# A decoder layer with eight experts: the first expert's weights split in the attention stage, no GpSimd drain between the stages, context values by half rows

## The chip, the cores and the metric

The kernel runs on one core of a Trainium2 chip. A core has five engines, each with its own instruction stream: TensorE (PE in the profile; its weight loads are PEld), VectorE (DVE), ScalarE (ACT), GpSimd (POOL) and SyncE (SP), which here only issues DMAs. They wait for each other by semaphores. The metric is the device time of one execution in microseconds (us): 1263.66 us before, the median of 3 runs (1262.08 to 1265.37).

## The reference

The input is x, 16 sequences of 256 tokens of 256 channels, f32. Three residual parts follow one another, each after a layer norm:

1. attention within windows of 8 tokens, 16 heads of 16 channels, the sequence shifted by 4, with a relative bias;
2. cross-attention of 16 heads of 64 channels to a context of 77 rows of 192 channels per sequence;
3. a mixture of 8 experts: each token goes to the one expert with the highest router logit.

```python
qkv = xw @ w_qkv + b_qkv                      # windows of 8 tokens
attn = softmax(q @ k.T * 16**-0.5 + bias); out = (attn @ v) @ w_proj + b_proj
k = context @ Wk; v = context @ Wv            # [77,192] @ [192,1024]
attn = softmax((x @ Wq) @ k.T * 64**-0.5); out = (attn @ v) @ Wo + bo
top1 = argmax(softmax(x @ router_w + router_b))
h = x @ w1[i] + b1[i]; a, g = split(h)        # w1[i]: [256, 2048]
y = (a * sigmoid(g)) @ w2[i] + b2[i]          # w2[i]: [1024, 256]
out = out + where(top1 == i, y, 0)
```

## The kernel before

The program has two stages, each one `Block`, that is five instruction streams that start together and meet at a barrier at the end. [...]

**The first stage** (`trunk`) takes the 16 sequences in 4 groups of 4. The windows of a group lie one on each of the 128 partitions, 8 tokens a window. The scores and values of the window attention are not matmuls: for each of the 8 queries an engine multiplies q (or the probabilities) by all 8 keys (or values) into a tile of 2048 numbers per partition (`make_product`, L275), and DVE sums the tile (`sum_scores` L808, `sum_values` L837). In later groups GpSimd makes all products, in three tiles. In the opening, window group 0, DVE makes those of even queries, in `xw`, and GpSimd those of odd queries (`POOL_FIRST`), in `tmp1`: two tiles, and the semaphore `consumed` says how many have been summed.

Beside it PE, in the opening, turns the context of two sequences at a time (`turn_context` L1121), makes their keys (`keys`, L1128) and their values (`context_values`, L1139). The context has 192 channels, so a value is two matmuls over the partitions: channels 0 to 127, and channels 128 to 191 with the rest of the 128 rows zero, which GpSimd clears at L412 to L414. The results go over ACT (`pair_kept`, L638) to memory, and SP loads the keys and values of a sequence when it is due (`load_keys`, L308; `load_values`, L311). ACT rounds the keys (`round_keys`, L656) ahead of the normed tokens `xn` (L616) in its stream. PE turns the window outputs (`output_turn`, L1095) two queries at a time, as soon as these are summed, and then projects them (`project`, L1108).

Each turn of `turn` handles one sequence: scores, values, four turned outputs `o2T` (ACT, L675), output projection, router logits (`logits`), queries for the next and the maxima of their scores (`maxima`, L865). The last group has no windows to prepare. SP loads the first expert's weights into `staged` before it (L380 to L383). Each sequence ends with `store_tokens` (L495) and `scatter_ids` (L483), which scatters token numbers into the list of each expert (`ids`).

**The second stage** (`experts`) works on 23 tiles of 256 tokens; the first four take the first tile of experts 0 to 3. Weights come in three pieces of 1 MB (`w1` in two, `w2`), are staged, and are split into a high and a low part: ACT copies (`high_part`, L1706), DVE subtracts (`low_part`, L1637). SP reads the ids of a tile, GpSimd gathers its tokens (`gather`, L1536) into `xs`, which DVE clears first (L1633) because rows without a token aren't written. PE turns them (`turn_tokens`, L1779), then runs three matmuls for each product. `locate` (L1601) is a list of small DVE steps that finds which expert the tiles after the eighth belong to; SP waits for it. The tiles run in a loop (`tiles`, L1455) with the next tile's preparation inside. Scattered results are waited for by SP at L1525.

## Time and profile before

| | us |
|---|---|
| median of 3 runs | 1263.66 |
| the profiled execution | 1264.1 |
| its span, first to last instruction | 1262.3 |
| PE busy | 1150.2 (91%) |
| DVE busy | 845.1 (67%) |
| POOL busy | 656.2 (52%) |
| ACT busy | 603.3 (48%) |

The times of the stages below are microseconds from the start of the span. PE is the engine that is busy most, and its idle time lies in a few stretches: the first 41 us, some 9 us around 140, 24.6 us between the stages, 6.6 us near 865 and 12 us at the end. A busy share is an average; what a change is worth is read at the wait that ends last in its place. A row of the timeline shows in brackets how long the engine had been idle before, and what ended the wait. The profile infers the releaser, and where it names an engine that had long been done, it was another.

### The profile page before, as it was taken

To read this page: it belongs to the slowest core of one execution; us is meant where nothing else is said; L and a number is where in the kernel's file an instruction comes from. 1 tells how busy PE (TensorE), PEld (TensorE's weight loads), DVE (VectorE), ACT (ScalarE), POOL (GpSimd) and SP (SyncE) were. 2 spreads that over 40 slices of the span, in tenths; PEclk is the share of its full clock that TensorE was granted. 3 is DMA by queue.
4 is the path that set the end of the run, shared out by engine and by line. 5 is a ranking of instruction groups with operands and counts; after the bars stand their busy time and mean duration, and the time that the engine had idled before them with its cause. 6 is when DMAs were issued, how large, how long until landed. Compare 5 with 4: busy or idle time off the path is not lost. (4 is left out here: it accounts for less than half of the span.)

```text
span 1262.3 us, 22231 instructions
## 1 busy us (share of the span) xinstructions
PE 1150.2 (91%) x8064; PEld 974.3 (77%) x8064; DVE 845.1 (67%) x1501; ACT 603.3 (48%) x1003; POOL 656.2 (52%) x542
## 2 busy tenths in 40 slices
PE   4999789999998999999999999627999999999996
PEld 2666457777777777677777888527999999999995
DVE  3678356777648776577773444338788888888983
ACT  1243332445514545334455544226666676666672
POOL 6347307666538575377765221351555655555551
PEclk9999899999999999999999999858999999999998
DMA  8432301111220111201124111144666766666650
GB/s 184 133 121 105 109 20 44 46 29 46 36 61 19 36 44 25 51 13 44 29 82 115 28 34 37 33 143 144 223 236 219 242 220 231 228 209 203 219 185 1
DMA packets 95383, 133.47 MB, mean 106 GB/s; under 512 B 42394, under 2 KB 76908, under 8 KB 89411
## 3 DMA queue, kind: packets, MB, share of 16 engines
q1 hardware_dynamic: 79299, 111.30, 28.1%
q0 software_dynamic: 16000, 21.07, 6.2%
q8 instruction: 51, 0.84, 0.3%
q14 instruction: 33, 0.27, 0.1%
HBM read 113.04 MB, written 24.73 MB: 109 GB/s over the span
## 5 line engine op out<-in xcount | busy, mean ns | idle before, releaser
L1792 PE MATMUL psH<-xhigh,whigh 128*128 128x256 f32 x736 | 209.2, 284 | 8.0 <-DVE wlow L1640 6.6
L1792 PE MATMUL psH<-xlow,whigh 128*128 128x256 f32 x736 | 206.7, 281 | 0.0
L1792 PE MATMUL psH<-xhigh,wlow 128*128 128x256 f32 x736 | 206.6, 281 | 0.0
L1640 DVE TENSOR_TENSOR wlow<-staged,whigh 128x2048 fp32r<-128x2048 f32 x69 | 158.1, 2293 | 0.0
L1709 ACT ACTIVATE whigh<-staged 128x2048 fp32r<-128x2048 f32 x69 | 132.3, 1919 | 44.6 <-DMA staged<-in_L_ffn_w 27.9
L1792 PEld LDWEIGHTS psH<-xhigh,whigh 128*128 128x128 f32 x736 | 141.1, 192 | 8.9 <-issue 6.8
L1295 PEld LDWEIGHTS psD<-vo,pT 128*128 128x128 f32 x1024 | 123.9, 192 | 24.1 <-issue 20.5
L1295 PE MATMUL psD<-vo,pT 128*128 128x128 f32 x1024 | 134.0, 278 | 6.9 <-issue 5.2
L1792 PEld LDWEIGHTS psH<-xlow,whigh 128*128 128x128 f32 x736 | 140.0, 190 | 0.0
L1792 PEld LDWEIGHTS psH<-xhigh,wlow 128*128 128x128 f32 x736 | 139.7, 190 | 0.0
L1534 POOL TENSOR_TENSOR idle<-e_less 128x1 f32<-128x1 f32 x42 | 49.8, 1185 | 170.6 <-DMA ids_now<-ids 86.6
L1154 PE MATMUL psA<-xT,wq 128*128 128x256 f32 x512 | 123.1, 389 | 0.7 <-ACT xT L629 0.7
L1723 ACT ACTIVATE sig<-psH,b1s 128x256 f32<-128x256 f32 x184 | 77.0, 470 | 76.2 <-PE psH L1792 76.1
L869 DVE TENSOR_REDUCE nm<-psD 128x4 bf16<-128x308 f32 x128 | 61.2, 478 | 76.0 <-PE psD L1167 72.5
L453 POOL TENSOR_TENSOR ve<-mv,eps 128x2 f32<-128x2 f32 x32 | 6.2, 195 | 199.3 <-DVE mv L928 131.4
L715 ACT ACTIVATE pT<-psA 77x512 f32<-77x512 f32 x128 | 76.0, 594 | 69.2 <-PE psA L1277 66.7
L1154 PEld LDWEIGHTS psA<-xT,wq 128*128 128x128 f32 x512 | 94.7, 193 | 16.6 <-ACT xT L629 5.4
L675 ACT ACTIVATE o2T<-psA 128x512 f32<-128x512 f32 x64 | 38.2, 597 | 141.5 <-PE psA L1305 140.9
L1652 DVE SCALAR_TENSOR_TENSOR gated<-psH,b1s,sig 128x256 f32<-128x256 f32 x184 | 80.2, 477 | 37.2 <-ACT sig L1723 36.5
L1804 PE MATMUL psY<-whigh,ghigh 128*128 128x256 f32 x368 | 102.8, 279 | 1.1 <-DVE ys L1667 0.7
L1804 PE MATMUL psY<-whigh,glow 128*128 128x256 f32 x368 | 102.2, 278 | 0.0
L1804 PE MATMUL psY<-wlow,ghigh 128*128 128x256 f32 x368 | 102.2, 278 | 0.0
(218 smaller groups left out, 2676.9 us busy)
## 6 DMA issues: line engine op xcount, KB each, us to landing
staged<-in_L_ffn_w SPq DMA_DIRECT2D x69, 1024.0 KB, 5.2
tokens<-out_rows POOLq DMA_DIRECT2D x32, 256.0 KB, 7.2
kT<-k_cols SPq DMA_DIRECT2D x16, 308.0 KB, 2.9
vo<-v_rows SPq DMA_DIRECT2D x16, 308.0 KB
xb<-in_x SPq DMA_DIRECT2D x32, 128.0 KB
b2s<-in_L_ffn_b SPq DMA_DIRECT2D x23, 128.0 KB
k_cols<-qT SPq DMA_DIRECT2D x4, 616.0 KB
v_rows<-pT SPq DMA_DIRECT2D x4, 616.0 KB
```

Source lines behind the costliest of these rows:

```text
L675: then(act, nc.scalar.activation(o2T[:, 2 * m:2 * m + 2, :].rearrange("p u n -> p (u n)"), ps, copy), a_done, value)
L715: then(act, nc.scalar.activation(pT[0:CTX, u % 4, :], ps[0:CTX, :], ACT.Exp, scale=D2 ** -0.5), a_done, value)
L869: then(dve, nc.vector.tensor_reduce(nm[:, t, 4 * m:4 * m + 4], ps[:, 0:4 * CTX].rearrange("p (h k) -> p h k", h=4), axis=X, op=ALU.max, ne ...
L1154: ins = mm(ps[:, u * N:(u + 1) * N], wq[:, c, (2 * q + u) * P:(2 * q + u + 1) * P], xT[:, c, :], start=c == 0, stop=c == KC - 1)
L1295: ins = mm(ps[:, m * P:(m + 1) * P], pT[:, (2 * w + m % 2) % 4, (m // 2) * N + t * P:(m // 2) * N + (t + 1) * P], vo[:, 4 * w + m, :], sta ...
L1534: nc.gpsimd.tensor_tensor(idle[:, i:i + 1], e_less_8[:, 0:1], e_less_8[:, 0:1], ALU.add)
L1640: tt(wlow[par][:, i, :], staged[:, i, :], whigh[par][:, i, :].bitcast(F32), ALU.subtract)\
L1652: ins = nc.vector.scalar_tensor_tensor(gated[:, q % 2, c, :], psH[:, q % 2 * PAIR + c, 0, :], b1s[:, par, q * PAIR + c:q * PAIR + c + 1], ...
L1709: nc.scalar.activation(whigh[par][:, i, :], staged[:, i, :], ACT.Copy).then_inc(w_high[i], 1)
L1723: ins = nc.scalar.activation(sig[:, q % 2, c, :], psH[:, q % 2 * PAIR + c, 1, :], ACT.Sigmoid, bias=b1s[:, par, k:k + 1])
L1792: ins = mm(psH[:, q % 2 * PAIR + c, part, :], lhs, rhs, start=i == 0, stop=i == len(passes) - 1)
L1804: ins = mm(psY[:, half, 0:C], lhs[:, q, c, half * P:(half + 1) * P], rhs[par][:, KC, k * C:(k + 1) * C], start=k == 0 and i == 0, stop=k = ...
```

## The change

Nine edits:

1. Two spaces of three 8 KB columns, `trunk_space`, hold what the first stage needs only up to its last group (`xw`, `tmp1`, `wk`, `wv`, `xnT`, `wqkv`); `first_high` and `first_low` of the first expert lie in the same memory. `ctx` and `relbias` lie in `xs_space`, later `xs`.
2. In the last group's first three turns ACT copies a piece of the first expert to `first_high`, after the third `o2T`, and DVE subtracts it after the logits and clears a part of `xs_space`.
3. Behind the last turn SP loads the second expert's three pieces.
4. `no_gpsimd_drain=True` for both blocks: the drain of GpSimd goes at the end of both stages. The drains of the other engines and the barrier stay.
5. Window group 0 has three product tiles, the third in `oT`; DVE's sums are in another order. PE waits for all sums of group 0 before it turns outputs, since ACT writes them to `oT`.
6. Context values: the 64 last channels of `Wv` are loaded twice, to rows 0 to 63 and 64 to 127, and ACT writes the turned context's last channels to both. The second matmul of a value covers 64 rows, for one half of the columns the lower, for the other the upper, alternating (`both_halves`). GpSimd's two clears go.
7. Second stage: `locate` is first on DVE, its constants are first on GpSimd, and the clears of `xs` are gone.
8. SP loads the biases ahead of the ids.
9. The second expert's first piece is copied first on ACT; what split the first expert is gone.

```diff
-        first_products = [xw[:], tmp1[:]]
+        first_products = [xw[:], tmp1[:],
+                          oT[:].rearrange("p k b i w -> p (k b i w)").rearrange("p (i c) -> p i c", i=WS)]
-        block = st.enter_context(nc.Block())
+        block = st.enter_context(nc.Block(no_gpsimd_drain=True))
...
-            return first_products[i % 2] if n == 0 else products[(n * TMP_ITEMS + i) % 3]
+            return first_products[i % 3] if n == 0 else products[(n * TMP_ITEMS + i) % 3]
...
-            eng.wait_ge(consumed, item + 1 if n == 0 else item)
+            if item > 0:
+                eng.wait_ge(consumed, item)
...
-            sp.dma_start(wv[0:CTXD - P, 1, :], Wv[P:CTXD, :]).then_inc(ctx_in, 16)
+            sp.dma_start(wv[0:D2, 1, :], Wv[P:CTXD, :]).then_inc(ctx_in, 16)
+            sp.dma_start(wv[D2:P, 1, :], Wv[P:CTXD, :]).then_inc(ctx_in, 16)
...
             turn(NG - 1, False)
+            for i in range(KC):
+                sp.wait_ge(w_split[i], 1)
+                sp.dma_start(staged[:, i, :], w1[1, i * P:(i + 1) * P, :]).then_inc(w_in[i], 16)
+            sp.wait_ge(w_split[KC], 1)
+            sp.dma_start(staged[:, KC, :].rearrange("p (k n) -> p k n", k=HC),
+                         w2[1].rearrange("(k p) n -> p k n", p=P)).then_inc(w_in[KC], 16)
...
-                then(act, nc.scalar.activation(ctxT[0:CTXD - P, i % 2, 1, :], ps[0:CTXD - P, 2 * CTX:4 * CTX], copy),
-                     a_done, value)
+                nc.scalar.activation(ctxT[0:D2, i % 2, 1, :], ps[0:D2, 2 * CTX:4 * CTX], copy)
+                then(act, nc.scalar.activation(ctxT[D2:P, i % 2, 1, :], ps[0:D2, 2 * CTX:4 * CTX], copy), a_done, value)
...
                         output_turned(n, 3)
+                    if not more and b < 3:
+                        act.wait_ge(w_in[b], 16)
+                        nc.scalar.activation(first_high[:, b, :], staged[:, b, :], copy).then_inc(w_high[b], 1)
                     output2_turned(3, j, b, last)
...
                         logits("LOG", j, b, last)
+                    if not more and b < 3:
+                        dve.wait_ge(w_high[b], 1)
+                        tt(first_low[:, b, :], staged[:, b, :], first_high[:, b, :].bitcast(F32), ALU.subtract)\
+                            .then_inc(w_split[b], 1)
+                        nc.vector.memset(xs_space[:, b], 0.0)
+                        if b == 2:
+                            nc.vector.memset(xs_space[:, 3], 0.0)
...
+            def both_halves(ps, lhs, rhs, out):
+
+                for k in range(2):
+                    mm(out(ps[k], k), lhs(0, k, slice(0, P)), rhs(0, k, slice(0, P)), start=True, stop=False)
+                for k in range(2):
+                    rows = slice(k * D2, (k + 1) * D2)
+                    yield mm(out(ps[k], k), lhs(1, k, rows), rhs(1, k, rows), start=False, stop=True)
+
             def context_values(i):
-                for n in range(4):
-                    ps = freeA(f"V{n}.{i}", -1, -1)
-                    q, half = n // 2, n % 2
-                    for c in range(KC):
-                        ins = mm(ps[0:CTX, :], ctxT[:, i % 2, c, q * CTX:(q + 1) * CTX],
-                                 wv[:, c, half * 512:(half + 1) * 512], start=c == 0, stop=c == KC - 1)
-                    ins.then_inc(a_full, 1)
+                for q in range(2):
+                    ps = [freeA(f"V{2 * q + half}.{i}", -1, -1) for half in range(2)]
+                    for ins in list(both_halves(
+                            ps, lambda c, k, rows: ctxT[rows, i % 2, c, q * CTX:(q + 1) * CTX],
+                            lambda c, k, rows: wv[rows, c, k * 512:(k + 1) * 512],
+                            lambda bank, k: bank[0:CTX, :])):
+                        ins.then_inc(a_full, 1)
...
             pe.wait_ge(weights, 16 * N_WEIGHTS)
+            pe.wait_ge(consumed, 2 + TMP_ITEMS)
             for k in range(4):
                 output_turn(0, k)
...
-            for t in range(DEPTH):
-                nc.vector.memset(xs[:, t], 0.0).then_inc(xs_cleared, 1)
...
-            low_part(0, 0, 0)
-            low_part(0, 0, 1)
+            locate()
             low_tokens(0, 0)
             dve.wait_ge(bias_in[0], 32)
             gate(0, 0, 0)
-            low_part(0, 0, 2)
+            low_part(1, 1, 0)
             gate_low(0, 0)
             low_tokens(1, 1)
             gate(0, 0, 1)
-            low_part(1, 1, 0)
             gate_low(0, 1)
-
-            locate()
```

How the instructions stand. DVE in the opening, from its first product of window group 0, before:

```order
L288 TENSOR_TENSOR xw<-staged 128x2048
L812 TENSOR_REDUCE probs<-xw 128x8x16
L812 TENSOR_REDUCE probs<-tmp1 128x8x16
L288 TENSOR_TENSOR xw<-staged 128x2048
L812 TENSOR_REDUCE probs<-xw 128x8x16
L812 TENSOR_REDUCE probs<-tmp1 128x8x16
```

and after (`trunk_space0` holds `xw`, its first column, and `tmp1`, its second; `oT` is the third tile):

```order
L300 TENSOR_TENSOR trunk_space0<-staged 128x2048
L832 TENSOR_REDUCE probs<-trunk_space0 128x8x16
L300 TENSOR_TENSOR oT<-staged 128x2048
L832 TENSOR_REDUCE probs<-trunk_space0 128x8x16
L832 TENSOR_REDUCE probs<-oT 128x8x16
L300 TENSOR_TENSOR trunk_space0<-staged 128x2048
L832 TENSOR_REDUCE probs<-trunk_space0 128x8x16 x2
L300 TENSOR_TENSOR trunk_space0<-staged 128x2048
```

A product is now made ahead of the sum of GpSimd's, so that DVE goes from sum to sum while GpSimd multiplies.

ACT in the turn of the third sequence of the last group, before and after:

```order
L629 ACTIVATE xT3<-psA 128x512
L675 ACTIVATE o2T<-psA 128x512
L715 ACTIVATE pT<-psA 77x512 x2
L675 ACTIVATE o2T<-psA 128x512 x3
L616 ACTIVATE xn<-x1,nb2,rs2 128x256 x2
L629 ACTIVATE xT<-psA 128x512
```

```order
L692 ACTIVATE o2T<-psA 128x512
L732 ACTIVATE pT<-psA 77x512 x2
L692 ACTIVATE o2T<-psA 128x512 x2
L761 ACTIVATE first_high<-staged 128x2048
L692 ACTIVATE o2T<-psA 128x512
L633 ACTIVATE xn<-x1,nb2,rs2 128x256 x2
L646 ACTIVATE xT<-psA 128x512
```

The copy to `first_high` stands between the third and the fourth `o2T`.

DVE at the start of the second stage, from the first subtraction to the head of `locate`, before:

```order
L1640 TENSOR_TENSOR wlow0<-staged,whigh0 128x2048 x2
L1645 TENSOR_TENSOR xlow<-psT,xhigh 128x512
L1652 SCALAR_TENSOR_TENSOR gated<-psH,b1s,sig 128x256 x2
L1640 TENSOR_TENSOR wlow0<-staged,whigh0 128x2048
L1660 TENSOR_TENSOR glow<-gated,ghigh 128x512
L1645 TENSOR_TENSOR xlow<-psT,xhigh 128x512
L1652 SCALAR_TENSOR_TENSOR gated<-psH,b1s,sig 128x256 x2
L1640 TENSOR_TENSOR wlow1<-staged,whigh1 128x2048
L1660 TENSOR_TENSOR glow<-gated,ghigh 128x512
L1604 TENSOR_TENSOR cmp<-counts,k_tiles 128x120
L1606 TENSOR_REDUCE ntiles<-cmp 128x8
```

and after, from the last step of `locate` to the end of what stands ahead of the loop:

```order
L1667 CAST tile_rowi<-tile_row 128x15
L1680 TENSOR_TENSOR xlow<-psT,xhigh 128x512
L1687 SCALAR_TENSOR_TENSOR gated<-psH,b1s,sig 128x256 x2
L1675 TENSOR_TENSOR wlow1<-staged,whigh1 128x2048
L1695 TENSOR_TENSOR glow<-gated,ghigh 128x512
L1680 TENSOR_TENSOR xlow<-psT,xhigh 128x512
L1687 SCALAR_TENSOR_TENSOR gated<-psH,b1s,sig 128x256 x2
L1695 TENSOR_TENSOR glow<-gated,ghigh 128x512
```

Three subtractions for the first expert and the 23 steps of `locate` no longer stand between the tokens and the loop.

## Rows read from the trace of the kernel before

**Rows 1.** Busy time by stretch: span, engines in order, clock, DMA share, GB/s

```profile
0.00:41.40 41.40, 25.26 (x81) 15.64 (x82) 16.34 (x39) 4.45 (x9) 21.45 (x42) 1.00 0.85 202
41.40:134.20 92.80, 92.44 (x426) 55.95 (x424) 74.76 (x31) 37.13 (x82) 54.85 (x9) 1.00 0.28 100
```

**Rows 2.** Timeline, DVE and POOL, score products: start, us, engine, line, operation, shapes

```profile
45.46 6.60 DVE L288 TENSOR_TENSOR xw<-staged 128x2048 f32<-128x2048 f32 x1 [2.89 <-DMA rb_b<-in_L_ffn_router_b]
...
56.73 2.29 DVE L288 TENSOR_TENSOR xw<-staged 128x2048 f32<-128x2048 f32 x1
56.84 6.56 POOL L288 TENSOR_TENSOR tmp<-staged 128x2048 f32<-128x2048 f32 x1 [6.93 <-DVE probs L812]
```

**Rows 3.** Timeline, DVE and POOL, end of scores, and the values

```profile
84.04 1.22 DVE L820 SCALAR_TENSOR_TENSOR probs<-probs,relbias 128x1024 f32<-128x1024 f32 x1
...
94.33 3.87 DVE L288 TENSOR_TENSOR xw<-staged,probs 128x2048 f32<-128x2048 f32 x1
94.43 7.46 POOL L288 TENSOR_TENSOR tmp<-staged,probs 128x2048 f32<-128x2048 f32 x1 [12.82 <-DVE probs L834]
...
131.87 2.29 DVE L842 TENSOR_REDUCE staged<-tmp 128x256 f32<-128x2048 f32 x1 [1.43 <-POOL tmp L288]
```

**Rows 4.** Timeline, PE: the last pair's context values, and the first projection

```profile
126.31 7.03 PE L1144 MATMUL psA<-wv,ctxT 128*77 128x512 f32 x16
...
137.35 3.47 PE L1115 MATMUL psD<-wproj,oT 128*128 128x256 f32 x8 [1.07 <-ACT oT L604]
```

**Rows 5.** Timeline, PE and its weight loads: 64-row score matmuls in a later turn

```profile
718.90 0.28 PE L1277 MATMUL psA<-nmT,head_row 64*77 64x256 bf16 x2
...
719.44 0.28 PE L1277 MATMUL psA<-nmT,head_row 64*77 64x256 bf16 x2
...
719.64 0.42 PEld L1176 LDWEIGHTS psA<-ident,out_rows 128*128 128x128 f32 x4 [0.30 <-issue]
```

**Rows 6.** Timeline, ACT: where the two ways of the opening meet

```profile
144.79 1.09 ACT L616 ACTIVATE xn<-x,nb,rs 128x256 f32<-128x256 f32 x2
```

**Rows 7.** Timeline, ACT and DVE, third turn of the last group

```profile
765.52 0.60 ACT L675 ACTIVATE o2T<-psA 128x512 f32<-128x512 f32 x1 [2.46 <-PE psA L1305]
...
775.09 0.99 DVE L869 TENSOR_REDUCE nm<-psD 128x4 bf16<-128x308 f32 x2 [5.02 <-PE psD L1167]
```

**Rows 8.** The page, costliest groups: busy and mean ns, idle before

```profile
L1709 ACT ACTIVATE whigh<-staged 128x2048 fp32r<-128x2048 f32 x69 | 132.3, 1919 | 44.6 <-DMA staged<-in_L_ffn_w 27.9
```

**Rows 9.** Line 137, the first block's end: ns min/median/max, start

```profile
L137 POOLq DRAIN  x1: 10279/10279/10279, 819.0 to 819.0; - x1
```

**Rows 10.** The last scatter of ids, issued at 820.50: its landing

```profile
DMA to landing us min/median/max: 7.7/7.7/7.7
```

**Rows 11.** Timeline, all engines, start of the second stage

```profile
829.77 0.91 DVE L1633 MEMSET xs<- 128x1024 f32 x1 [11.37 <-PEq L137]
...
833.84 2.29 DVE L1640 TENSOR_TENSOR wlow<-staged,whigh 128x2048 fp32r<-128x2048 f32 x1
...
841.64 1.11 PE L1775 MATMUL psT<-ident,xs 128*128 128x128 f32 x4 [24.55 <-DMA xs<-tokens,ids_now]
```

**Rows 12.** Tile `xs`, 800 to 860 us: gathers, ns min/median/max, and landings

```profile
L1542 POOL DMA_INDIRECT xs<-tokens,ids_now x8: 1009/1062/3070, 832.6 to 847.0; - x8
...
DMA to landing us min/median/max: 3.5/4.0/7.6
```

**Rows 13.** Timeline, DVE and PE: `locate`, first and last, and PE's stop

```profile
858.93 0.28 DVE L1604 TENSOR_TENSOR cmp<-counts,k_tiles 128x120 f32<-128x120 f32 x1
...
864.18 0.17 DVE L1630 CAST tile_rowi<-tile_row 128x15 int32<-128x15 f32 x1
...
867.91 0.58 PE L1792 MATMUL psH<-xhigh,whigh 128*128 128x256 f32 x1 [6.56 <-DVE wlow L1640]
```

**Rows 14.** Lines 1399 and 1525, the end: ns, first and last start

```profile
L1399 POOLq DRAIN  x1: 9870/9870/9870, 1252.2 to 1252.2; - x1
...
L1525 SPq EVENT_SEMAPHORE  x2: 17/22/28, 1255.3 to 1255.4; - x2
```

More of the change, by code:

```diff
@@ L887, in _ @@
             window_divide(0)
[L888 to L890 removed]
+            for i in range(0, WS, 2):
+                make_product(dve, nc.vector.tensor_tensor, 0, WS + i, i, True, s.done)
+                if i > 0:
+                    sum_values(0, i - 1)
                 sum_values(0, i)
+            sum_values(0, WS - 1)
             start_sequence(-1, -1)
@@ L1389, in _, with experts @@
             turn(NG - 1, False)
-def experts(nc, w1, w2, b2, out, tokens, tokens_stored, ids, scattered, ident, staged, w_in, counts, e_less_8,
+def experts(nc, w1, w2, b2, out, tokens, tokens_stored, ids, scattered, ident, staged, first_high, first_low, xs_space,
+            w_in, w_high, w_split, counts, e_less_8,
             b1_cols, b1_stored):
@@ L1423, in experts @@
         tile_rowi = sb("tile_rowi", [P, NT], I32)
-        whigh = [sb(f"whigh{i}", [P, PIECES, HC * C], F32R) for i in range(2)]
-        wlow = [sb(f"wlow{i}", [P, PIECES, HC * C], F32R) for i in range(2)]
+        whigh = [first_high, sb("whigh1", [P, PIECES, HC * C], F32R)]
+        wlow = [first_low, sb("wlow1", [P, PIECES, HC * C], F32R)]
         b1s = sb("b1s", [P, 2, 2 * HC])
@@ L1580, in _ @@
                 .then_inc(first_located, 1)
+            pool.wait_ge(tokens_stored[0], 32 * (B // 2 + 1))
+            pool.wait_ge(tokens_stored[1], 32 * (B // 2 + 1))
+            for t in range(DEPTH):
+                gather(t, 0, first=True)
+                if t == 1:
+                    for i in range(2):
+                        for half in range(2):
+                            nc.gpsimd.dma_start(ys[0:1, i, half, :], b2[0:1, :]).then_inc(y_stored[i], 16)
             def tile(t, slot, turn):
```

86 lines of the change are left out of this document (39 added, 47 removed).

## The prediction

> **What bounds the kernel now.** I first read the table of stretches, then the timeline of each stretch in which TensorE (PE) is not busy, because a change of this kind can only pay where the last thing to end is one that it touches. From 160 us to the end of the attention stage PE is busy for all but a few per cent and every other engine waits for it, so nothing there is for sale. Four places are.
>
> The first is the opening, 41.4 to 144.8 us. PE is busy for 92.4 of 92.8 us at the full clock [rows 1], with the keys and values of the context, while VectorE (DVE) and GpSimd (POOL) do the attention of the first windows. Both streams end almost together: the last context values at 126.31 + 7.03 = 133.3 [rows 4], the last sum of the windows at 131.87 + 2.29 = 134.2 [rows 3]. Behind the first lies the way of the keys (stored, loaded back, rounded by ScalarE, ACT), behind the second the projection at 137.35 [rows 4] and the first layer norm; they meet at ACT's `xn`, 144.79 [rows 6]: 11.5 us after the context, and 10.6 after the windows. To save anything, both must shrink.
>
> The second is the change of stage. POOL's drain runs 10.28 us from 819.0, so to 829.3 [rows 9]; no engine enters the experts before. PE then waits for the first gathered tokens until 841.64 [rows 11]. The third is PE's stop of 6.56 us before 867.91 for `wlow` of the second expert [rows 13]. The fourth is the end: the last output has landed when SyncE (SP) passes its wait at 1255.3 to 1255.4, but POOL's drain of 9.87 us, begun at 1252.2, holds the end to 1262.1 [rows 14].
>
> **The windows at the opening.** Before, POOL's products share one tile with no slack, so DVE waits for each. One DVE product takes 2.29 us, and POOL's, begun 0.11 later, 6.56 [rows 2]: POOL stands still until 59.02 and then needs 4.4. The two kinds of product exclude each other, and the first to start holds; DVE's very first took 6.60, one of POOL's and its own [rows 2]. Played through with three tiles, the score part is 6.6 for the first product, then three products and eight sums at 2.29 + 0.03: 6.6 + 25.5 = 32.1 us; POOL needs 2.3 + 4.4 = 6.7 per product and DVE's turn is 6.95, so POOL keeps up. Before it was 84.04 - 45.46 = 38.6 [rows 2, 3]: 6.5 saved. The value part has four products of 3.87 and eight sums, 34.2 us, and one collision: DVE's second product comes 6.2 us in, and POOL holds until 7.5 [rows 3]: 35.5 against 134.2 - 94.3 = 39.8, so 4.4 saved. The softmax between (84.0 to 94.3) stays.
>
> Against it: a second copy of 256 KB of `Wv` goes into a queue that already moves 202 GB/s up to 41.4 us [rows 1], and DVE starts when the weights behind it have landed: 256 KB / 202 GB/s = 1.3 us later. Windows end at 134.2 - 6.5 - 4.4 + 1.3 = 124.6. The new wait holds PE's turning of the outputs until then, and behind it queue all four turns and the projection, which had been half done before the last sum: 0.7 us for the turns that no longer overlap, 0.5 for turns at half clock after an idle PE, both estimates from the projection's own eight matmuls, 3.47 us at 137.35 [rows 4], twice a full-clock one. So `xn` comes by this way at 124.6 + 10.6 + 1.2 = 136.4.
>
> **The context values.** Eight matmuls of 512 columns take 7.03 us a pair. Four are now 64 rows high, in pairs on the two halves of the array. The score matmuls show what that gives: four records of such 64-row f32 and two bf16 pass in 719.44 - 718.90 = 0.54 us [rows 5], half of what 256 columns each, one after the other, would take (1.07). So 3.4 of the 7.03 becomes 1.7: 1.7 x 8 = 13.7 us. Each change between 128 and 64 rows costs something: after the last 64-row matmul of 719.44 streams out at 719.55, the next 128-row weight load starts at 719.64, and its engine was idle 0.30 [rows 5]. There are 32 such changes; at 0.1 they cost 3.2, at 0.30 they cost 9.6. I take 0.1, the part that lies beyond the streaming. The context then ends at 133.3 - 13.7 + 3.2 = 122.8, the keys are ready at 134.3, before `xn` could start by the windows' way. The opening gives 144.8 - 136.4 = 8.4. Its bounds: with 0.30 per change the keys decide, 129.2 + 11.5 = 140.7, and 4.1 remain; with no cost of changes, no delay of the DMAs and no collision, the context's way decides too, 119.6 + 11.5 = 131.1, and 13.7.
> The Trainium skill (TensorEngine Tiling, Key Properties) says that changing the tiling mode drains TensorE. By that rule each of the 32 changes would cost the rest of what streams; the trace's gap of 0.09 to 0.30 us bears it out, and the two ends above are what it makes of the sum.
>
> **The last turns.** ACT copies 1.92 us [rows 8] in each of the first three, between the third and fourth `o2T`, where it was idle 2.46 [rows 7]. DVE subtracts 2.29 [rows 11] and clears 0.91, together 3.4 with issue, in the third turn two clears, 4.4, where it was idle 5.02 before the maxima [rows 7]. Both fit, by 0.5 and 0.6 us. Cost 0; were the cover gone, at most three times 1 us. The three loads of the second expert come after the last `vo` load on SP's queue, so nothing queues behind them before the barrier. The barrier itself remains; only POOL's drain goes.
>
> **The change of stage.** The ids cannot be read before the last scatter lands, 820.5 + 7.7 = 828.2 [rows 10], so the drain's removal gives not 8 us but 829.3 - 828.2 = 1.1. The four clears go, but the first was done at 830.7 [rows 11], before the ids were there: nothing. Of the eight gathers one took 3.07 where the others take 1.06 [rows 12]: it is the second half of the first tile, issued beside DVE's subtraction of 833.84 [rows 11], now gone: 2.0. It landed 7.6 after its issue, against 3.5 of the best [rows 12]; of these 4.1, 2.0 are the same issue, and the other 2.1 I put down to the megabytes of weights that were loading beside it; I take 1.8. Sum 1.1 + 2.0 + 1.8 = 4.9; bounds 2.0 (only the first, and half of the second) and 5.9.
> The Trainium skill (SBUF — State Buffer, "SBUF: two separate sides") gives the lock of a DVE instruction with two SBUF inputs only against a GpSimd one that reads SBUF, and names perf-mode instructions as what starves a GpSimd DMA. By it the 3.07 would stay, and the sum be 2.0 us less; the row of 3.07 beside a plain two-input subtraction speaks against it.
>
> **The second expert.** The 23 small steps that place the tiles stand on DVE from 858.93 to 864.35, and PE's 6.56 us stop follows from them [rows 13]. They now run while the scatter lands. The third gate and the `wlow` behind it come 5.4 earlier at most; ACT's copy of the second piece is still in front of its sigmoid, so I take 5.3 and leave PE 1.2 us of the stop. After it PE ran half speed for 3.4 us; if the shorter stop keeps the clock up, 1.7 more. Bounds 4.0 and 8.2.
>
> **The end.** SP's wait, then the barrier: 1262.3 - 1255.4 - 0.4 = 6.5. Bounds 6.0 and 6.7.
>
> **Sum.** 8.4 + 0 + 4.9 + 5.3 + 6.5 = 25.1 us off the profiled execution's 1264.1 (span 1262.3, 1.8 around it; the median of the runs is 1263.7, so the same to 0.4): 1239.0. Lowest terms, 4.1 + 2.0 + 4.0 + 6.0 = 16.1, give 1248; highest, 34.5, give 1229.6.
>
> **Rivals.** *The context stays the bound* (0.10). If two 64-row matmuls into two different PSUM banks don't overlap, PE's stream does not shrink and pays 32 changes: 3.2 us later instead of earlier. For it: their 512 columns and 77-column weights are nowhere in the trace in this form. Against: the 0.54 us of [rows 5], also two banks. Time: 1264.1 - 16.7 + 3.2 = 1250.6.
> *The end drain moves, it does not go* (0.08). What the drain waits for may be waited for behind the last instruction, outside the span. For it: 9.87 us is far more than the landing needs, so it is some fixed work. Against: nothing in the trace asks for it. Time 1239.0 + 6.5 = 1245.5.
> *The locks go the other way* (0.05): POOL arrives first at DVE's products again and again, each costing up to 4.3 us as at 45.46; two more such would make 1247.
> *Slower: PE falls to its lower clock in the context* (0.02). Place: the eight pairs, 77 us of work after the change; mechanism: half of the array idle in a fourth of it, with short stops at changes. All of it at 1.2 GHz instead of 2.4 would end the context at 122.8 + 77.3 = 200.1 and have `xn` at 211.6, 66.8 us later than before; less the other 16.7, the time is 1314. It decides from the point where the context ends 16.7 us later than 133.3, that is with 27 of the 77 us lost, a third of it at the lower clock. Against: the trunk, which has 64-row matmuls in every turn, is at 1.00, as is this stretch [rows 1].
>
> **How the numbers follow.** Forecast 0.75, rivals as given. 0.3% is 3.8 us, about what a measurement of this kernel can tell. Only the last rival lies above 1260, so faster 0.96, same 0.02, slower 0.02. Range 1231 to 1248: the forecast's own bounds but for the last of each side, and of the rivals the end drain and the locks; the context rival is mostly left out.
>
> **What would show it.** Right: POOL's two drains gone or under 0.5 us; `xn` of the first sequence near 136.4; the first expert turn of tokens 8.5 us after the last scatter has landed (13.4 before); PE's stop near the second expert under 2 us; span end 0.4 us after the last output landed. Wrong: PE's context loop longer than 10.5 us a pair, a wait of DVE's maxima for `first_low` or of `o2T` for `first_high` in the last turns, a gather of 3 us, a last scatter that lands later than 7.7, or a total that differs from the span by more than 1.8.

## The result, and the profile after

The changed kernel takes 1249.1 us (median of 5 runs, 1247.2 to 1250.4) against 1264.7 for the kernel before (5 runs): a ratio of 0.9873, 95% interval 0.9857 to 0.989. It is faster, by 15.6 us and not by 25; 1249.1 lies 1.1 us above the predicted range. The profiled execution has a span of 1247.7 us.

The term by term comparison needs only the times at which a few instructions start. First the opening, all timelines (start, us, engine, line): the last sum of the windows; the context values, where two pairs begin (after, then the same two before) and the last 64-row matmuls; ACT's rounding of the keys and its first `xn`, and GpSimd's last step before `xn`; and ACT's second `xn`, after and before.

```profile
124.09 2.29 DVE L862 TENSOR_REDUCE staged<-trunk_space 128x256 f32<-128x2048 f32 x1
```

```profile
57.98 1.88 PE L1173 MATMUL psA<-trunk_space,ctxT 128*77 128x512 f32 x4
...
68.26 1.88 PE L1173 MATMUL psA<-trunk_space,ctxT 128*77 128x512 f32 x4
...
124.11 1.09 PE L1176 MATMUL psA<-trunk_space,ctxT 64*77 64x512 f32 x4
```

```profile
58.35 7.03 PE L1144 MATMUL psA<-wv,ctxT 128*77 128x512 f32 x16
...
69.73 7.03 PE L1144 MATMUL psA<-wv,ctxT 128*77 128x512 f32 x16
```

```profile
135.56 1.45 ACT L678 ACTIVATE kTb<-kT 64x616 bf16<-64x616 f32 x2 [5.28 <-DMA kT<-k_cols]
135.68 0.20 POOL L473 TENSOR_TENSOR nb<-zeros,nb 128x2 f32<-128x2 f32 x1
137.05 1.09 ACT L633 ACTIVATE xn<-x,nb,rs 128x256 f32<-128x256 f32 x2
...
200.50 1.09 ACT L633 ACTIVATE xn<-x,nb,rs 128x256 f32<-128x256 f32 x2 [2.49 <-POOL nb L473]
```

```profile
205.98 1.09 ACT L616 ACTIVATE xn<-x,nb,rs 128x256 f32<-128x256 f32 x2 [2.49 <-POOL nb L456]
```

The windows end at 124.09 + 2.29 = 126.4 (134.2 before, [rows 3]), the context at 125.2 (133.3, [rows 4]), `xn` starts at 137.05 (144.79, [rows 6]): 7.7 us earlier. The windows' way was ready for `xn` at 135.9, when `nb` was; `xn` waited for the keys, whose rounding ends at 137.0. A pair of sequences takes 68.26 - 57.98 = 10.28 us, before 69.73 - 58.35 = 11.38. But the second `xn` starts 63.45 after the first; before it was 205.98 - 144.79 = 61.19. So 2.3 of the 7.7 are lost again within one turn.

The last turns: ACT's copy before the fourth `o2T`, and DVE's wait before the maxima (timelines).

```profile
757.85 1.91 ACT L761 ACTIVATE first_high<-staged 128x2048 fp32r<-128x2048 f32 x1
760.22 0.60 ACT L692 ACTIVATE o2T<-psA 128x512 f32<-128x512 f32 x1 [0.46 <-PE psA L1345]
```

```profile
769.78 0.99 DVE L889 TENSOR_REDUCE nm<-psD 128x4 bf16<-128x308 f32 x2 [0.48 <-PE psD L1206]
```

Where ACT and DVE were idle for 2.46 and 5.02 [rows 7] they are idle for 0.46 and 0.48, and still PE is what they wait for. The last `ids` scatter is issued at 815.24 (820.50 before, [rows 10]), 5.3 us earlier, where the second `xn` was 5.5 earlier: at most 0.2 us is lost in all the turns between, the last ones with them.

The stage change: the last scatter of `ids` (landing), the gathers, and PE's waits in the second stage (line, releaser, sum, times, longest).

```profile
L508 POOL DMA_INDIRECT ids<-id_now,rowi x1: 969/969/969, 815.2 to 815.2; - x1
...
DMA to landing us min/median/max: 8.5/8.5/8.5
```

```profile
L1580 POOL DMA_INDIRECT xs_space<-tokens,ids_now x8: 994/1005/1092, 826.6 to 838.0; - x8
...
DMA to landing us min/median/max: 3.4/3.5/3.6
```

```profile
PE psT L1803 <- DMA xs_space<-tokens,ids_now: 19.7, 1, 19.7
...
PE psH L1820 <- DVE wlow L1675: 1.3, 1, 1.3
```

Now the loop of the tiles. Rows are the transposes that open a tile (timeline; the fourth before, then the fourth and the twentieth after), and then 100 us from the middle of the loop in both kernels, before first.

```profile
886.40 0.60 PE L1775 MATMUL psT<-ident,xs 128*128 128x128 f32 x4
```

```profile
870.18 0.60 PE L1803 MATMUL psT<-ident,xs_space 128*128 128x128 f32 x4
...
1151.09 0.60 PE L1803 MATMUL psT<-ident,xs_space 128*128 128x128 f32 x4
```

```profile
1000.00:1100.00 100.00, 100.00 (x867) 100.00 (x866) 84.83 (x99) 68.13 (x94) 57.53 (x43) 1.00 0.67 225
```

```profile
1000.00:1100.00 100.00, 100.00 (x845) 100.00 (x844) 81.32 (x98) 65.45 (x92) 56.03 (x39) 1.00 0.66 219
```

PE is busy for all of the 100 us in both, at the full clock in both, waits for nothing in either, with the DMA engines alike; and it gets through 867 matmuls before and 845 after. A tile takes (1151.09 - 870.18) / 16 = 17.56 us; before, 17.13 wherever PE didn't wait. Busy share, waits and clock, the three things that I looked at in this stretch, show no difference: only the count does. From here to the landing of the last output it costs 8.0 us.

The end: SP's wait for the last output.

```profile
L1563 SPq EVENT_SEMAPHORE  x2: 17/22/28, 1247.1 to 1247.2; - x2
```

Passed at 1247.2, span 1247.7: there is no drain of GpSimd (before 1255.4 and 1262.3, [rows 14]). A drain is an instruction that an engine passes at the end of a block; before the change GpSimd's took 9.87 us here, though the last output had landed 6.7 us before it ended.

| | predicted, us | measured, us |
|---|---|---|
| opening, to the first `xn` | -8.4 | -7.7 |
| from there to the last scatter | 0 | +2.5 |
| last scatter to first tokens on PE | -4.9 | -4.9 |
| the second expert | -5.3 | -6.1 |
| the loop of the tiles | 0 | +8.0 |
| the end | -6.5 | -6.4 |
| span | -25.1 | -14.6 |

The second expert is the time between the first tokens of the first tile and those of the fourth: 886.4 - 841.64 = 44.8 before, 870.18 - 831.50 = 38.7 after.

### The profile page after: what moved, and what is told of

It is laid out like the page before. It is cut to its first block and busy times, and to the rows that moved or that the text cites. A ratio compares the mean times of both kernels' runs of the same rounds, so it can differ in the third digit from the quotient of the medians.

```text
span 1247.7 us, 22257 instructions
## 1 busy us (share of the span) xinstructions
PE 1150.9 (92%) x8064; PEld 976.7 (78%) x8064; DVE 841.5 (67%) x1501; ACT 604.6 (48%) x1011; POOL 653.9 (52%) x540
## 5 line engine op out<-in xcount | busy, mean ns | idle before, releaser
L300 POOL TENSOR_TENSOR trunk_space<-staged 128x2048 f32<-128x2048 f32 x27 | 128.4, 4754 | 86.1 <-DVE staged L821 35.2
L300 POOL TENSOR_TENSOR trunk_space<-staged,probs 128x2048 f32<-128x2048 f32 x27 | 116.5, 4316 | 28.1 <-DVE probs L854 17.9
L1820 PE MATMUL psH<-xhigh,first_high 128*128 128x256 f32 x384 | 110.7, 288 | 1.5 <-DVE xlow L1680 1.5
L1820 PE MATMUL psH<-xlow,first_high 128*128 128x256 f32 x384 | 109.5, 285 | 0.0
L1820 PE MATMUL psH<-xhigh,first_low 128*128 128x256 f32 x384 | 109.4, 285 | 0.0
L1820 PE MATMUL psH<-xhigh,whigh 128*128 128x256 f32 x352 | 99.7, 283 | 1.3 <-DVE wlow L1675 1.3
L1820 PE MATMUL psH<-xlow,whigh 128*128 128x256 f32 x352 | 99.0, 281 | 0.0
L1820 PE MATMUL psH<-xhigh,wlow 128*128 128x256 f32 x352 | 98.7, 280 | 0.0
L1597 POOL DMA_INDIRECT out<-ys,ids_now x46 | 88.2, 1918 | 11.3 <-issue 11.3
L1123 PE MATMUL psW<-trunk_space 128*128 128x512 f32 (+1 forms) x256 | 89.5, 493 | 2.2 <-ACT trunk_space L605 2.2
```

Source lines behind the costliest of these rows:

```text
L300: done(tensor_tensor(o, a, w, ALU.mult))
L1123: ins = mm(dst, xnT[:, c, i, :], wqkv[:, c, cols], start=c == 0, stop=c == KC - 1)
L1597: nc.gpsimd.indirect_dma_start(out=out.rearrange("b n c -> (b n) c"), out_offset=bass.IndirectOffsetOnAxis(ap=ids_now[:, slot, half:half + ...
L1820: ins = mm(psH[:, q % 2 * PAIR + c, part, :], lhs, rhs, start=i == 0, stop=i == len(passes) - 1)
```

## The experiments

Ratios are to the kernel before, measured beside each kernel (1264.7 to 1265.2). Differences to 1249.1 are between medians taken at different times; medians of the kernel before differ by 0.5 us between these times. Traces are of one execution each.

**1. Where the operands lie, by itself.** The program's matmuls are the same, but their operands' addresses moved: `first_high`, `first_low` begin at bytes 41920 and 66496 of a partition, where `whigh0`, `wlow0` began at 43488 and 92640; `xhigh` moved from 160416 to 160448. By the remainder by 128: weights before 96 and tokens 32; after, weights 64 (even tiles) and 96 (odd tiles), tokens 64. A kernel that only multiplies tested that:

```diff
+PLACES = {
+    "bef_a": (43488, 92640, 160416, 164512, lambda *a, **k: ...),   # L32
+    "bef_b": (68064, 117216, 162464, 166560, ...),                  # L33
+    "aft_a": (42016 - 96, 66496, 160448, 164544, ...),              # L34
...
+            for t in PLACES.values():
+                for q in range(4):
+                    hidden(t, q)
+                for q in range(4):
+                    down(t, q)
```

> This kernel leaves out the whole reference and writes zeros; its time says nothing. TensorE runs, one group after another, the matmul pattern of the experts (96 for the hidden layer, 48 for the product with w2, 128x128 weights, 256 columns of fp32r) on one buffer of zeros, at the byte offsets that the tiles have in the kernel before (43488, 92640, 160416 for the even tiles, 68064, 117216, 162464 for the odd ones) and after (41920, 66496, 160448; 109024, 133600, 162496), and at offsets with one of the two shifted. The four pairs are run again with VectorE and ScalarE busy. Theory (places): the distance between two matmuls depends on where the operands lie: 113 ns for before's even tiles, 118 for its odd ones, 120 and 118.5 for after's, without any other engine at work, and a shift of 32 or 96 bytes of one operand moves it. Rival (load): all groups show one distance, or differ only while VectorE and ScalarE work.

The groups' rows (busy us of 96 matmuls; L32 to L35 are the four pairs of places, L43 after's even tiles with weights and tokens shifted back to 96 and 32, L48 to L51, the four pairs again beside DVE and ACT, took 11.5, 11.1, 11.7 and 11.5):

```profile
L34 PE MATMUL psH<-field 128*128 128x256 f32 x96 | 11.7, 283 | 0.0
...
L35 PE MATMUL psH<-field 128*128 128x256 f32 x96 | 11.5, 281 | 0.0
...
L32 PE MATMUL psH<-field 128*128 128x256 f32 x96 | 11.5, 281 | 0.0
L43 PE MATMUL psH<-field 128*128 128x256 f32 x96 | 11.1, 276 | 0.0
...
L33 PE MATMUL psH<-field 128*128 128x256 f32 x96 | 11.1, 276 | 0.0
```

With nothing else at work, the groups take 11.1, 11.5 or 11.7 us, and the same again with DVE and ACT busy: the rival (load) falls. After's two pairs of places came as expected. Before's two came the other way round: its even tiles' places took 11.5 and its odd tiles' 11.1, though both have the remainders 96 and 32. L43, after's even tile (L34, 11.7) with both operands 32 bytes off, took 11.1. But L42 and L44, also at 96 and 32, took 11.5, so this experiment alone doesn't say which addresses give the lower time.

**2. The same in the two kernels.** Unused tiles shift the experts' tiles and, as the first of them stands ahead of the first stage's tiles, many of those too; no instruction is changed:

```diff
+        keep("pad0", [P, 8])
         with ExitStack() as shared:
...
+        sb("pad1", [P, 24])
         whigh = [first_high, sb("whigh1", [P, PIECES, HC * C], F32R)]
...
+        sb("pad2", [P, 24])
         xhigh = sb("xhigh", [P, 2, KC, ET], F32R)
```

> The changed kernel with three unused tiles of 32, 96 and 96 bytes, so that the weights and split tokens of the experts have the remainder by 128 that they had in the kernel before (weights 96, tokens 32; changed kernel: first expert's weights 64, tokens 64). Theory (places, by remainder): a tile of the loop takes 17.13 us again instead of 17.55, 19 tiles, 8 us less: 1241. Rival (places by something coarser, or load): 17.55 a tile as before, 1249.

> The kernel before with unused tiles of 96, 32, 96, 32 and 32 bytes among its expert tiles, so that remainders by 128 are those of the changed kernel (even weights 64, odd weights 96, tokens 64). Theory (places, by remainder): 17.55 us a tile, 8 us more than before: 1272. Rival: no change, 1264.

Measured: 1240.5 us (ratio to before 0.9819, interval 0.9801 to 0.9837) and 1272.8 us (1.0063, 1.0046 to 1.008). Changed kernel with pads, then kernel before with pads:

```profile
1000.00:1100.00 100.00, 100.00 (x863) 100.00 (x862) 85.35 (x99) 66.56 (x94) 57.05 (x42) 1.00 0.64 219
```

```profile
1000.00:1100.00 100.00, 100.00 (x847) 100.00 (x846) 81.74 (x98) 65.31 (x92) 55.95 (x39) 1.00 0.63 218
```

863 and 847 matmuls, where without the pads it was 845 and 867. The loop, from the tokens of the fourth tile to the landing of the last output, takes 369.5 us with pads (1238.1 - 868.6) where it took 377.0, and 376.2 with pads in the kernel before (1264.1 - 887.9) where it took 369.0: 7.5 less and 7.2 more. Addresses are all that the edit changes, so they are the cause of the loss in the loop, in both directions. The whole times moved by 8.6 and 8.0, close to the expected 8 in part by luck: 1.6 and 1.5 of these lie ahead of the fourth tile.

**3. Which remainders.** Groups without the second product between them, first at four places that share the remainders 96 and 32, then all pairs:

```diff
+    "00_odd": (68064, 117216, 162464, 166560, ...),     # L32; L32 to L43 all have 96 and 32
+    "01_even": (43488, 92640, 160416, 164512, ...),
...
+    "12_w0_x0": (65536, 114688, 160384, 164480, ...),   # L44; to L59 all pairs, L60 to L75 again, backwards
```

> This kernel leaves out the whole reference and writes zeros. TensorE runs groups of 96 matmuls in the pattern of the experts' hidden layer, nothing else running. First 12 groups at four places that all have remainder 96 (weights) and 32 (tokens) by 128, some twice in a row, in the order odd, even, even, odd, odd, pad, even, far, pad, far, even, odd; then all pairs of the remainders 0, 32, 64, 96 of weights and tokens, once up and once down at other base addresses. Theory (remainders only): the pair of remainders sets the distance; 96 with 32 has two levels, 113 and 118, that alternate from change to change whatever the place is, and repeat where the place is not changed. Rival (whole address): each of the four places has its level each time (even and far 118, odd and pad 113). For the grid: weights at 64 are 120 with every remainder of the tokens, weights at 96 with tokens at 64 118, and if the alignment to 32 but not 64 is what makes it fast, 32 does as well as 96.

```profile
L58 PE MATMUL psH<-field 128*128 128x256 f32 x96 | 11.7, 282 | 0.0
...
L57 PE MATMUL psH<-field 128*128 128x256 f32 x96 | 11.0, 276 | 0.0
L32 PE MATMUL psH<-field 128*128 128x256 f32 x96 | 11.0, 276 | 0.0
```

All twelve groups at 96 and 32 took 11.0 us: the rival (whole address) falls for this pair, but so does my guess of two levels that change with the place. The grid, busy us of 96 matmuls, first pass / second pass at other bases:

| weights \ tokens | 0 | 32 | 64 | 96 |
|---|---|---|---|---|
| 0 | 11.6 / 11.5 | 11.4 / 11.6 | 11.1 / 11.5 | 11.5 / 11.5 |
| 32 | 11.7 / 11.7 | 11.6 / 11.6 | 11.4 / 11.4 | 11.1 / 11.1 |
| 64 | 11.5 / 11.5 | 11.7 / 11.7 | 11.6 / 11.5 | 11.4 / 11.6 |
| 96 | 11.4 / 11.4 | 11.0 / 11.0 | 11.7 / 11.7 | 11.6 / 11.6 |

My guess that alignment to 32 but not 64 is fast is wrong too: 32 with 32 and 96 with 96 took 11.6. The lowest times, 11.0 and 11.1, all lie where the remainders of weights and tokens differ by 64 bytes; no other difference has one. A difference of 64 is not enough: 64 with 0 took 11.5 both times, and 0 with 64 took 11.1 and then 11.5, so for some pairs the remainders don't say all. The pair 32 and 96, 11.1 both times, can be tried in the kernel:

```diff
+        keep("pad0", [P, 24])
...
+        sb("pad1", [P, 24])
...
+        sb("pad2", [P, 24])
```

> The changed kernel with three unused tiles of 96 bytes each, so that the experts' weights all have remainder 32 by 128 and the split tokens 96. Theory (the difference of the two remainders counts, 64 is the fast one): as with 96 and 32, 17.13 to 17.20 us a tile, 1240.5. Rival (only the pair 96 and 32 is fast): 17.5 a tile, 1249.

1241.9 us (0.9818, 0.9795 to 0.984), 864 matmuls in the same 100 us. So 96 and 32 is not the only pair that gives the loop its lower time. Of the pairs that differ by 64 only these two were tried in a kernel; the other two took 11.5 at least once in the grid.

**4. The opening.** Each half of it undone, and both:

```diff
-                for q in range(2):
-                    ps = [freeA(f"V{2 * q + half}.{i}", -1, -1) for half in range(2)]
...
+                    for c in range(KC):
+                        ins = mm(ps[0:CTX, :], ctxT[:, i % 2, c, q * CTX:(q + 1) * CTX],
+                                 wv[:, c, half * 512:(half + 1) * 512], start=c == 0, stop=c == KC - 1)
```

> The changed kernel with the context values as before (second matmul over 128 rows, upper rows zero). My theory (two ways, each ends the opening): the keys' way takes over, first xn at 144.8 instead of 137.05, 7.7 us; since TensorE is then busy until 133, the 2.2 us that its first turn lost to the lower clock come back: 1249.1 + 5.5 = 1254.6. Rival (the windows alone set it): no change, 1249.

```diff
-            return first_products[i % 3] if n == 0 else products[(n * TMP_ITEMS + i) % 3]
+            return first_products[i % 2] if n == 0 else products[(n * TMP_ITEMS + i) % 3]
...
-            if item > 0:
-                eng.wait_ge(consumed, item)
+            eng.wait_ge(consumed, item + 1 if n == 0 else item)
...
-            pe.wait_ge(consumed, 2 + TMP_ITEMS)
```

> The changed kernel with two product tiles, the old order and the turns waiting for their own sums in window group 0. My theory: windows end at 134.2 again, xn at 144.8, 7.7 us back; TensorE is still idle from 123 on, so the lower clock stays: 1256.8. Rival (the half rows alone carry the opening, the third tile nothing): 1249.

> The changed kernel with both undone, the context values and the product tiles. My theory: the same opening as before, xn at 144.8 and the second xn 61.2 after it, so the same time as with full values alone: 1254.6. Rival (gains add up part by part): 1249 + the sum of what the two single undoings cost, over 1260.

Measured: 1255.43, 1255.47, 1255.32 us (ratios 0.9924, 0.9908 to 0.9941; 0.9929, 0.9912 to 0.9945; 0.9926, 0.991 to 0.9943). Their first `xn`, in this order:

```profile
145.12 1.09 ACT L634 ACTIVATE xn<-x,nb,rs 128x256 f32<-128x256 f32 x2
```

```profile
144.58 1.09 ACT L631 ACTIVATE xn<-x,nb,rs 128x256 f32<-128x256 f32 x2 [3.78 <-POOL nb L471]
```

```profile
144.40 1.09 ACT L632 ACTIVATE xn<-x,nb,rs 128x256 f32<-128x256 f32 x2
```

Either half undone costs as much as both, 6.2 to 6.4 us: each alone is worth nothing that these runs can tell. The rivals (one part carries it, the parts add) fall. Which way ends last differs: with the two tiles the keys are rounded by 140.8 and `xn` waits 3.78 us for the windows; with the full values `nb` is ready at 143.4 and `xn` waits for the keys until 145.1. The two ways are not separate there: DVE waited 10.1 us for ACT's exponential, which stands behind the context's copies, so the slower context held back the windows as well. With the two tiles I expected 1.3 us more, since PE is idle in parts there; the second `xn` came 61.6 after the first all the same, so that part of my reading of the clock was too simple.

**5. The clock in the first turn.** Granted clock (third column from the end) from PE's return; before, then after:

```profile
150.90:155.90 5.00, 5.00 (x29) 4.22 (x28) 1.32 (x3) 2.67 (x6) 0.00 (x0) 0.95 0.00 0
165.90:175.90 10.00, 8.84 (x53) 5.93 (x54) 4.76 (x14) 3.78 (x7) 0.00 (x0) 1.00 0.01 3
```

```profile
143.20:148.20 5.00, 5.00 (x22) 4.17 (x21) 0.96 (x2) 2.17 (x4) 0.00 (x0) 0.76 0.01 2
158.20:168.20 10.00, 8.01 (x44) 6.11 (x45) 4.16 (x12) 3.78 (x7) 0.14 (x1) 0.83 0.03 9
```

Both kernels run at 0.50 in the first 5 us. After the change the half clock lasts longer (0.76 against 0.95 in the second 5 us), and it falls a second time, to a mean of 0.83, in 10 us that had 1.00 before. In the experiment PE has something to do before `xn`:

```diff
             project(-1, -1, 0)
+            for k in range(46):
+                nc.tensor.transpose(psW[:, k % 2, 0:P], ident[:], ident[:])
```

```profile
132.50 5.50 PE L1242 MATMUL psW<-ident 128*128 128x128 f32 x46
```

```profile
137.50:142.50 5.00, 4.25 (x24) 3.65 (x23) 0.00 (x0) 1.68 (x3) 2.53 (x2) 1.00 0.47 98
```

The clock is 1.00, and the second `xn` starts 195.62 - 136.34 = 59.3 us after the first. 4.3 us less in all, where the rival expected none. So the first fall comes of what PE did ahead of it. The second fall, which is what the kernel before doesn't have, the transposes did not remove:

```profile
150.00:155.00 5.00, 4.67 (x30) 2.95 (x28) 2.77 (x17) 2.53 (x5) 1.85 (x2) 0.66 0.10 31
```

An estimate from the windows of the traces shows that the clock is still the whole loss. Count as lost PE's busy time times one minus the granted clock, us by us, from the first `xn` to the second: 2.3 us before, all in the first 12 us of the turn; 5.0 after, 3.3 there and 1.6 in the second fall; 1.6 with the transposes, all in the second fall. The turn without its lost time is 58.9 us before and 58.5 after, and 58.4 to 58.9 in the eight other kernels of this case without the transposes. Of these ten, the five with the first `xn` at 144.4 to 145.3 (the two of before, the three of experiment 4) have no second fall; the five with it at 136.3 to 137.1 have it. What sets it off is open: PE's longest wait near it is 1.8 us in both kernels.

**6. The second expert.** `locate` behind the first tokens again:

```diff
-            locate()
             low_tokens(0, 0)
...
             gate_low(0, 1)
+            locate()
```

> The changed kernel with the 23 steps that place the tiles behind the first tokens again, as before. My theory (my sum): TensorE's stop near the second expert is 6.6 us again instead of 1.3, 5.3 us back: 1254.4; if the clock falls in the longer stop, 1.7 more: 1256.1. Rival (the copies of the second expert set the stop): no change, 1249.1.

1255.05 us (0.9927, 0.9906 to 0.9947), PE's stop:

```profile
PE psH L1821 <- DVE wlow L1675: 5.0, 1, 5.0
```

6.0 us more in all, between my 5.3 and the 7.0 with the clock; the rival (the copies set the stop) falls. But the stop is 5.0 us and not 6.6, so it gives only 3.7 of the 6.0. The rest goes with the clock, 0.51 and 0.80 in the 10 us from 855, where the changed kernel has 1.00.

**7. The drains.**

```diff
-        block = st.enter_context(nc.Block(no_gpsimd_drain=True))
+        block = st.enter_context(nc.Block())
```

> The changed kernel with GpSimd's drain restored at the end of both stages. Theory (my sum): 1.1 us at the change of stage and 6.5 at the end come back, 1249.1 + 7.6 = 1256.7. Rival (drain hid nothing at the change, only the end counts): 1255.6; or the whole 10.3 + 9.9 us come back: 1269.

1258.0 us (0.9947, 0.9931 to 0.9964), 8.9 us more; the two drains, and SP's last wait:

```profile
L147 POOLq DRAIN  x1: 9906/9906/9906, 813.0 to 813.0; - x1
```

```profile
L1440 POOLq DRAIN  x1: 9863/9863/9863, 1246.1 to 1246.1; - x1
```

```profile
L1563 SPq EVENT_SEMAPHORE  x2: 17/22/28, 1249.2 to 1249.2; - x2
```

At the end the span goes on from 1249.2 to 1256.2, 7.0 against 0.5: 6.5 of the 8.9. At the stage change the first tokens are turned 833.13 - 814.5 = 18.6 us after the last scatter, 16.3 without the drain: 2.4, twice what I had. SP's rows show where the larger part lies (start, us, engine, line, DMA):

```profile
823.13 0.33 SPq L1524 DMA_DIRECT2D b2s<-in_L_ffn_b  x1
...
825.00 1.79 SPq L1530 DMA_DIRECT2D ids_now<-ids  x4
```

The four loads of the biases, which edit 8 put ahead of the ids, start when the drain is over and hold the ids back for 1.9 us; without the drain they lie in the wait for the scatter. So 2.4 is the price of a drain in the changed kernel. In the kernel before, the ids go first, and no run took its drain away alone.

**8. What comes of it.** Pads of experiment 2, transposes of experiment 5, and more of these at the head of the second stage:

```diff
+            for k in range(110):
+                nc.tensor.transpose(psH[:, 3, k % 2, 0:P], ident[:], ident[:])
             turn_tokens(0, 0, 0)
```

> The changed kernel with the unused tiles of 32, 96 and 96 bytes (1240.5), the 46 transposes behind the first projection, and 110 more on TensorE at the head of the second stage, where it waits 19.7 us and then runs 7 us at half clock. Theory: 2 to 5 us less in the first turn and up to 3.4 less in the first tile: 1233 to 1237. Rival (the clock falls at its own time): 1240.5; if the transposes outlast the waits, more.

1236.8 us (5 runs, 1236.4 to 1237.4; ratio 0.9782, 0.9767 to 0.9797): faster than both kernels. It is 3.7 under the pads alone, about what the first 46 transposes gave. The 110 gave nothing that shows in the first tile:

```profile
808.85 14.28 PE L1859 MATMUL psH<-ident 128*128 128x128 f32 x110 [2.12 <-PEq L148]
826.17 0.65 PE L1808 MATMUL psT<-ident,xs_space 128*128 128x128 f32 x4 [3.04 <-DMA xs_space<-tokens,ids_now]
```

```profile
826.10:833.60 7.50, 5.93 (x28) 5.70 (x29) 0.69 (x1) 0.60 (x1) 6.28 (x9) 0.55 0.50 145
```

They ended 3.0 us before the tokens came, and the first tile ran at a mean clock of 0.55, as it did without them (0.53). Whether 25 more of them would keep it was not tried. The second fall of experiment 5 is absent here: the clock is 1.00 from 130 to 170 us, and the second `xn` comes 59.0 after the first.

## Why the prediction was wrong

**The step that failed** is the list of places before the sum: "Four places are." It was drawn up from the stretches in which PE is not busy. The loop of the tiles, where PE is busy, is not among them, and the sum puts it at nothing without a reason. I read a busy PE as a PE whose speed is given. The loop has 19 rounds and some 2800 matmuls, and in its steady part the diff changes no matmul. But edit 1 moved their operands, and some 0.43 us a tile make the 8.0 us (experiments 1 to 3). With this term the same sum gives 1247; with the 2.5 up to the last scatter as well, 1249.5, the time of the profiled execution.

**The opening** came near in size, 8.4 predicted and 7.7 measured, and both parts were needed, as the argument of two ways said (experiment 4). But the prediction had the windows' way end last and the keys ready two us earlier, and it was the keys that ended it, at 137.0; the small difference is in part luck. On the windows' way, the scores took 75.9 - 46.2 = 29.7 us (32.1 played through), the values 126.4 - 91.1 = 35.2 (35.5). The softmax between them, which I took as given, didn't stay: 15.2 us instead of 10.3. DVE's row after the exponential, and ACT before it (timelines of after):

```profile
75.93 1.22 DVE L840 SCALAR_TENSOR_TENSOR probs<-probs,xs_space 128x1024 f32<-128x1024 f32 x1
...
86.92 1.94 DVE L850 TENSOR_REDUCE red<-probs 128x128 f32<-128x1024 f32 x1 [6.54 <-ACT probs L707]
...
91.14 3.88 DVE L300 TENSOR_TENSOR oT<-staged,probs 128x2048 f32<-128x2048 f32 x1
```

```profile
85.78 1.04 ACT L707 ACTIVATE probs<-probs 128x1024 f32<-128x1024 f32 x1
```

DVE waits 6.54 us for ACT's exponential (1.64 before), and ACT has it in its order behind the copies of a pair's values. The scores were done earlier, but the exponential was still tied to the pace of the context. So the windows end at 126.4 and not at 124.6, although DVE started only 0.7 us late instead of 1.3. Against that, the 1.2 us for PE's turns and projection never came: `nb` is ready 9.5 us after the windows, before 10.2, with the projection at 1.99 us instead of 3.47.

On the context's way the overlap is there: four 64-row records take 1.09 us. A pair of sequences takes 10.28 us where it took 11.38. Of the 1.7 that the overlap saves, 0.6 go into four changes between 128 and 64 rows, some 0.15 each, between my bounds of 0.1 and 0.3 and half as much again as I took: 1.6 us over the 32. The context also started 0.7 us late, of which 0.3 is ACT's third copy (edit 6), which the prediction had no term for. So it ended at 125.2 and not at 122.8. The rule of the Trainium skill (TensorEngine Tiling, Key Properties) that a change of the tiling mode drains TensorE agrees with a cost at each change, and the trace puts it at about 0.15 us.

**The clock** in the first turn was a term of 0 and measured +2.3, of the +2.5 up to the last scatter. I looked at the clock where PE stops longer (the second expert) and not at PE's return behind the opening. It was the smaller error.

**The last turns** cost 0, though only 0.46 and 0.48 us of slack were left, as worked out (0.5 and 0.6).

**The stage change** was right in sum, 4.9, and the parts can be read in the rows. From the first gather to the first tokens on PE it took 841.64 - 832.58 = 9.1 us before and 831.50 - 826.59 = 4.9 after, 4.1 less where the gather and the landings had 3.8: the gather of 3.07 us is gone (the longest now 1.09), and the tokens land 3.4 to 3.6 after their issue instead of up to 7.6. The subtraction beside that gather is gone too, which agrees with the reading that it held the gather up, but no run takes it away alone, and the weights that loaded beside it moved as well. From the scatter's landing to the reading of the ids it took 829.57 - 828.2 = 1.4 before and 0.1 after, 1.3 less where the drain had 1.1; the last scatter itself took 8.5 instead of 7.7 and took 0.8 back.

**The second expert**: the stop of PE is 1.3 us, as taken. The granted clock is 1.00 around it (850 to 860 us) where it was 0.66 before (861.6 to 871.6); I had the clock only as a bound, so it is 6.1 instead of 5.3. Experiment 6 divides the 6 us otherwise, 3.7 for the stop and the rest with the clock.

**The end**: 6.4, as predicted.

**The rivals**: none came. The one nearest in time, the context as the bound (1250.6), rests on 64-row matmuls that don't overlap, and is refuted by the 10.28 us of a pair and by `xn` at 137.05. The median of 1249 so agrees with a rival whose mechanism isn't there: the time alone would have confirmed the wrong story. The drain did go (6.4 at the end). The locks cost less than played through, as DVE's first product took 2.29 us and not 6.60. The granted clock in the context is 1.00.

## What to carry to other kernels

An edit that moves tiles in memory touches every instruction that reads them, in stages that the diff doesn't name: list the start addresses of the operands of the hottest matmuls before and after, and compare matmuls done per 100 us, since busy time, waits and clock can all be equal while a loop is 2.5% slower. Where two streams meet, a cut in one is worth nothing until the other is cut; read at the meeting point, in the trace after too, which of them came last. Where TensorE is idle ahead of a busy stretch, look at its granted clock behind it: work with no use, 5.5 us of it, bought 4.3 us here, and 14.3 us of it that ended 3.0 us too early bought none in the first tile. A drain costs what lies behind the last landing, and what then queues behind the drain, not its own length.

## What the runs showed of the hardware

- The distance between two 128x128 by 256-column fp32r matmuls, at the full clock and with no wait, depends on the addresses of its operands (on zeros): 96 took 11.0 us where weights and tokens differed by 64 in their remainder by 128, and 11.4 to 11.7 elsewhere (one such group 11.1 and again 11.5, and weights 64 with tokens 0 took 11.5 both times, so 64 is needed but doesn't suffice). DVE and ACT at work changed nothing. In the kernel the same loop, with other addresses only, took 369.5 us or 377.0.
- In experiment 1, with the product with w2 between them, groups at 96 and 32 took 11.1 and 11.5 in turn, in experiment 3 always 11.0. What sets the two levels is open; that the place of a matmul in the instruction stream counts was not tested.
- Two 64-row matmuls on the two halves of the array ran together (four records in 1.09 us), and a change between 128 and 64 rows cost some 0.15 us.
- The granted clock fell a second time some 20 us into the first turn, to 0.83 over 10 us, in the five kernels whose turn started at 136 to 137 us without transposes ahead of it, and in none of the five where it started at 144 to 145. Why is open.
- GpSimd's drain took 9.9 to 10.3 us in all four places where it stood; the kernels without it end 0.5 us behind the last landing.
